# Decoder kernel on one core: the key splits get their own signal, and seven moves in the queues of four engines around attention

## The reference

```
layer 0: causal attention, 16 heads of 128, biases   -> adjacency from ctx (top-k, sigmoid) -> ternary experts, top-1 of 32
layer 1: causal attention, 16 heads of 128, 4 key/value heads, rotary, head_scale -> cross attention with ctx -> 16 experts, top-4, and a shared one

q = rotary(x @ Wq); k = rotary(x @ Wk); v = x @ Wv           # layer 1
attn = softmax(causal(q k^T / sqrt(128))); out = (attn @ v * head_scale) @ Wo
```

## Time and profile before

| | before |
|---|---|
| median of 3 runs | 883.27 us (881.48 to 884.78) |
| the profiled execution: its own time | 881.88 us |
| its span | 880.1 us |
| TensorE busy | 795.0 us (90%), 4727 matmuls |
| VectorE, ScalarE, GpSimd busy | 578.0, 421.4, 500.4 us |
| mean granted TensorE clock | 0.965 |

### The profile page before, as it was taken

How to read it: one execution, slowest core, us unless ns; L and a number is a source line. 1 busy time by engine, 2 the same in 40 slices (tenths; PEclk the granted TensorE clock), 3 DMA queues, 4 the chain that set the end, 5 groups by cost and what they waited for, 6 DMA issues and landing times. The chain is left out here.

```text
span 880.1 us, 14575 instructions
## 1 busy us (share of the span) xinstructions
PE 795.0 (90%) x4727; PEld 681.2 (77%) x4733; DVE 578.0 (66%) x1659; ACT 421.4 (48%) x1193; POOL 500.4 (57%) x409
## 2 busy tenths in 40 slices
PE   7899999999999977594899999999987699999995
PEld 5678888888988866293678788888876488888884
DVE  4796967868668476333688788776726655554555
ACT  5164636546356546061376665765753633223232
POOL 4857287575768441603484566457512376777764
PEclk9999999999999998797999999999999799999998
DMA  6220702204225310564120111010001011111111
GB/s 205 73 96 1 239 20 78 96 1 144 72 73 168 96 54 20 168 157 103 61 74 5 54 54 55 1 55 25 25 1 38 13 38 51 52 38 54 38 40 48
DMA packets 58332, 59.09 MB, mean 67 GB/s; under 512 B 5393, under 2 KB 49313, under 8 KB 58273
## 3 DMA queue, kind: packets, MB, share of 16 engines
q1 hardware_dynamic: 57504, 56.24, 20.5%
q0 software_dynamic: 768, 2.10, 0.7%
HBM read 50.00 MB, written 8.32 MB: 66 GB/s over the span
## 5 line engine op out<-in xcount | busy, mean ns | idle before, releaser
L976 ACT ACTIVATE a_probs<-bank,a_neg_peak 128x128 f32<-128x128 f32 (+1 forms) x256 | 103.2, 429 | 100.5 <-DVE a_neg_peak L1094 100.5
L1004 ACT ACTIVATE a_probs<-a_probs,a_row_inv 128x128 f32<-128x128 f32 (+1 forms) x256 | 92.1, 454 | 6.2 <-DVE a_row_inv L1102 6.2
L1094 DVE CUSTOM_DVE_ANT_0 bank<-bank,causal 128x128 f32<-128x128 f32 (+1 forms) x256 | 82.5, 395 | 15.3 <-PE bank L837 15.3
L982 ACT ACTIVATE a_probs_t<-bank 128x512 f32<-128x512 f32 x96 | 54.1, 602 | 78.8 <-PE bank L857 78.8
L126 PE MATMUL bank<-a_wo_hi,a_ot_hi 128*128 128x256 f32 x256 | 74.6, 291 | 7.9 <-DVE a_ot_lo L1114 7.5
L876 PE MATMUL bank<-a_probs_t,a_vals 128*128 128x256 f32 x256 | 76.6, 381 | 2.7 <-DVE a_ot_lo L1114 2.0
L1814 POOL TENSOR_TENSOR d_h_lo<-d_h,d_h_hi 128x512 fp32r<-128x512 f32 x40 | 51.7, 1294 | 45.6 <-ACT d_h_hi L1934 32.0
L689 POOL TENSOR_TENSOR a_queries<-sim 128x512 f32<-128x512 f32 x32 | 41.5, 1298 | 60.1 <-DVE sim L1069 60.1
L2020 DVE TENSOR_TENSOR d_h<-d_silu,bank 128x512 f32<-128x512 f32 x40 | 27.5, 688 | 71.8 <-PE bank L128 70.5
L127 PE MATMUL bank<-a_wo_lo,a_ot_hi 128*128 128x256 f32 x256 | 73.0, 285 | 0.0
L128 PE MATMUL bank<-a_wo_hi,a_ot_lo 128*128 128x256 f32 x256 | 73.0, 285 | 0.0
(11 more groups left out here) (328 smaller groups left out, 2425.1 us busy)
## 6 DMA issues: line engine op xcount, KB each, us to landing
d_raw<-in_L_ffn_we_dram SPq DMA_DIRECT2D x48, 128.0 KB, 2.2
raw_k<-in_L_attn_w_k_dram SPq DMA_DIRECT2D x8, 512.0 KB, 6.4
raw_q<-in_L_attn_w_q_dram SPq DMA_DIRECT2D x8, 512.0 KB, 5.6
raw_v<-in_L_attn_w_v_dram SPq DMA_DIRECT2D x8, 512.0 KB, 7.2
raw_o<-in_L_attn_w_o_dram SPq DMA_DIRECT2D x8, 512.0 KB, 3.5
kv<-_L_ffn_expert_masks_dram SPq DMA_DIRECT2D x16, 256.0 KB, 3.1
kvt<-_L_ffn_expert_masks_dram SPq DMA_DIRECT2D x16, 256.0 KB, 3.1
raw_o<-in_L_attn_Wo_dram SPq DMA_DIRECT2D x8, 512.0 KB, 3.6
```

Source lines behind the costliest of these rows:

```text
L976: nc.scalar.activation(probs[s % 2][:, i, at:at + width], c.banks[i][:, at:at + width], ACT.Exp, bias=neg_peak[:, n:n + 1], scale=-1.0, ac ...
L982: nc.scalar.activation(probs_t[:, i * BANK:(i + 1) * BANK], c.banks[3 + (3 * s + i) % 2][:], ACT.Copy).then_inc(s_pt_free, 1)
L1004: last = nc.scalar.activation(part, part, ACT.Copy, scale=row_inv[:, s % 2, n + r:n + r + 1])
L1094: last = nc.vector.tensor_tensor_reduce(part, part, mask, -1.0, 3e38, ALU.add, ALU.min, neg_peak[:, n + r:n + r + 1])
```

## The change

1. Layer 1: the key part of a group is split first and alone, with a semaphore of its own, `s_split_k`; the key projection waits only for that.
2. Layer 1: the fourth value tile is projected before `scores(0)` and not behind `proj(1)`, and ScalarE evicts it before `exps(0)`.
3. Layer 1: in steps that still project, one transposed bankful comes before the next projection and two behind it; before it was two and one.
4. Layer 1, VectorE: the addition of the second output bank (u = 1) goes from the end of an odd step to behind `peaks` of the next (not at `TURN_STEP`).
5. Layer 1, VectorE: `sums` runs as two tiles in step 1 and two in step 3, between the two output banks, and no more behind steps 0 and 2; `norm3.apply` goes from the end of step 4 to step 5, behind `peaks(6)` and ahead of `pv(4)`.
6. Both layers, step 14: ScalarE takes the four q = 0 exponentials of step 15 before `pt(14)` and the other four behind `pv(14)`; VectorE takes `inverses(15)` behind `pv(14)`.
7. Both layers: `last_output` waits for the exponentials of the bank that it writes, not for all.

```diff
+        self.s_split_k = S("split_k") if self.rope else None
...
         for n, heads in (("k", min(self.KH, 2)), ("q", 2)):
+            if parts and self.rope:
+                self.split(pool, parts, self.s_split_k)
+                parts = []
...
-                    pe.wait_ge(s_split_proj, s + 1)
...
                         if rope and what == "k":
-                            pe.wait_ge(s_split_proj, group_of(s, what) * STEPS + 1)
+                            pe.wait_ge(weights.s_split_k, group_of(s, what) + 1)
+                        else:
+                            pe.wait_ge(s_split_proj, s + 1)
...
-                    pe.wait_ge(s_exp, PAIRS_OF_HEADS * NT)
                     pe.wait_ge(s_taken, taken("pv", LAST - 1 + (heads.stop - 1) // 2, (heads.stop - 1) % 2))
                     for u in range(2):
+                        pe.wait_ge(s_exp, LAST * NT + B + 2 * u)
...
-                    first_values(range(0, 3))
+                    first_values(range(0, NT // 2))
                 scores(0)
...
-                    first_values(range(3, 4))
...
-                    transposes(s, range(0, 2))
+                    first = 1 if rope and count else 2
+                    transposes(s, range(0, first))
                     proj(s + 2, range(0, min(count, 1)) if late else range(early, count))
-                    transposes(s, range(2, 3))
+                    transposes(s, range(first, 3))
...
-                early = 3 if rope else 0
+                early = NT // 2 if rope else 0
...
+                    if s == LAST - 1:
+                        exps(s + 1, range(0, 1))
                     pt(s)
-                    if s == LAST - 1:
-                        exps(s + 1)
...
-                    if s < LAST - 1 and late:
-                        exps(s + 1)
+                    if s < LAST and late:
+                        exps(s + 1, range(1 if s == LAST - 1 else 0, 2))
...
                     if s < LAST:
                         peaks(s + 1)
+                    if rope and s % STEPS == 0 and s not in (0, TURN_STEP + 1):
+                        output(s // STEPS - 1, 1, ring_bank("o", s // STEPS - 1, 1))
+                    if rope and s == NORM_STEP + 1:
+                        weights.norm3.apply(dve, 1, weights.s_norm3)
...
-                        if s < LAST and not (rope and count):
+                        if s < LAST - 1 and not (rope and count):
                             inverses(s + 1)
                     if not defers(s):
                         pv(s)
...
-                        if s < LAST and count < 3:
-                            inverses(s + 1)
+                    if s == LAST - 1 or s < LAST and late and count < 3:
+                        inverses(s + 1)
...
-                        for u in range(2):
+                        for u in range(1 if rope and s != TURN_STEP else 2):
                             output(s // STEPS, u, ring_bank("o", s // STEPS, u))
-                    if rope and s < NT // 2:
-                        weights.sums(dve, range(NT // 2 + s, NT // 2 + s + 1))
-                    if rope and s == NORM_STEP:
-                        weights.norm3.apply(dve, 1, weights.s_norm3)
+                    if rope and s % STEPS and s < NORM_STEP:
+                        weights.sums(dve, range(NT // 2 + s - 1, NT // 2 + s + 1))
```

More of the change, by code:

```diff
@@ L968, in _, with exps @@
             def _(act):
-                def exps(s):
-                    for q in range(2):
+                def exps(s, halves=range(2)):
+                    for q in halves:
                         for b in range(B):
```

## The result

The changed kernel takes **877.59 us** (median of 6 runs, 875.22 to 879.55); the kernel before, beside it, took 883.87 us (6 runs). The ratio is 0.9927, 95% interval 0.9905 to 0.9950: 6.3 us faster, between 4.4 and 8.4. The forecast was 879.9 us in a range of 876.5 to 883.2. The profiled execution has a span of 875.5 us and a time of its own of 877.31; before it was 880.1 and 881.88.

The account below looks back on a forecast made before the run. TensorE, busy for 90% of the span, was taken as the bound, with gains only where it stands still or runs at half clock. Terms summed to 3.35 us, giving 878.5, plus 1.39 to the median: 879.9 us, range 876.5 to 883.2.

Parts of the forecast that it names:

- The end of layer 1: Step 14, before last_output: wait falls from 3.42 to 1.7 us, clock kept; gain 2.85 us, 1.35 if the clock falls.
- The end of layer 0: End of layer 0's attention: GpSimd finishes last, so the next block begins 0.5 us earlier, bounds 0 and 0.7.
- Key first: Layer 1, steps 1, 3, 9, 11: waits for the query-weight split vanish; 1.7 us in the first two, 1.3 in the others.
- The start: Layer 1, before scores(1): the value tile only moves, wait grows from 1.50 to 3.0 us; gain 0, bounds -0.3 and 0.3.
- a rival with 0.7: Layer 1's start: the 3.0 us wait drops the clock too, costing about 0.7; counted inside the forecast's chance of 0.55.
- Steps 1 to 5: Layer 1: scores(6) comes 1.5 us earlier, step 5 gives it back; gain of all steps up to there 0.2 us.
- -1.5 for the clock: Step 5, behind pv(5): the wait grows from 2.00 to some 3.4 us; half clock costs 1.5, bounds 0 and 1.7.
- The 0.6 charged for the rotation of the keys: Layer 1's moved sums: the first tile runs into the key rotation, VectorE held until GpSimd's instruction ends; 0.6 us charged.
- The reading that VectorE is held by GpSimd's splits: Step 5: norm3.apply's four instructions each wait for one of GpSimd's splits; they took 5.76 us before the change.
- The other rivals of step 5: VectorE not held: 7.3 us gain, 876.0, chance 0.10; held for all of GpSimd's run: slower, 884.5, chance 0.07.
- The clock's rule: TensorE's waits in layer 1: one of 2.00 us left the clock alone, one of 3.42 us did not.
- The sum: Whole kernel: 2.85 + 0.5 + 1.3 + 0 + 0.2 - 1.5 = 3.35 us gained.

Follow-up runs that it names:

- the key's kernel: The kernel before with only the key split first and signalled by itself (item 1); ratio to the kernel before 0.9930.
- the half `keep`: The changed kernel with the first half of layer 0's keep moved ahead, into VectorE's idle time behind peaks(15); ratio to the kernel before 0.9918.
- the four with one part each: The kernel before with one part alone: items 6 and 7, ratio 0.9952; item 1, 0.9930; items 4 and 5, 1.0011; item 2, 1.0011.

## Why the prediction was right, point by point

**The end of layer 1** (2.85 forecast): the wait was to be 1.7 and is 1.61, the clock to be kept and is kept. `transposes(15)` win 2.97 us counted from scores(15), the block 3.22. Right. The runs show what the clock has in it: with the wait of 3.41 and no fall, in the key's kernel, the same stretch takes 23.08 us, so 1.4 of the 3.2 are the wait and 1.85 the clock.

**The end of layer 0** (0.5): 0.63, with GpSimd last, as the steps said. Right, and the half `keep` shows that it was GpSimd: it moves the block by 1.9 us more. The clock fell behind the block's wait, which the forecast didn't name, at no cost.

**Key first** (1.3 in steps 9 and 11): 1.89. The mechanism was right, and the term was sized by the waits alone. In steps 9 and 11 the waits were 1.3 us, and in each of the four steps the gain was about 0.28 more than the wait (1.11 in step 1, where the wait was 0.83). The rows show part of it: in an unbroken run a matmul starts 0.16 us before the record of the one ahead ends (in the key's kernel the key's first starts at 460.83, the query's last ends at 460.99), and behind a wait it doesn't.

**The start** (0, bounds -0.3 and 0.3): this step failed. The wait grew to 2.90 as forecast (3.0), but the clock fell behind it, and scores(1) to (2) lost 1.45 us. It was written down as a rival with 0.7, and a chance of its own inside the forecast; the price was twice that, since no slack of VectorE's chain took anything off. By the runs it happens 4 times in 6.

**Steps 1 to 5** (+0.2, and -1.5 for the clock): from scores(2) to scores(6) 1.92 us were won where 1.5 were forecast. They are the key's alone: the kernel with items 1, 6 and 7 wins 2.20 over the same stretch (54.67 us against 56.87), so the moved sums and additions, to which the forecast gave a part of the 1.5, cost 0.28 here. Counted from scores(2), `peaks(3)` comes 1.11 us earlier with the key and 1.44 with all items, and the addition moved behind it takes 0.68. The 0.6 charged for the rotation of the keys was right in size: L416 took 1.02 us beside it (465.08 to 466.10), where 0.42 is its time, and L418, the one the forecast had in mind, 0.48.

In step 5 `scores(6)` to `pv(5)` took 8.86 us (505.04 to 513.90), where 8.85 were worked out (506.15 to 515.0); L1313 took 4.39 us behind `peaks(6)`, within the "4 to 5 us". Net: 2.93 lost in step 5, 1.0 in all five steps, against 1.3 forecast. The reading that VectorE is held by GpSimd's splits was only argued; the kernel with `norm3.apply` out of their way shows it: 1.38 us for the same four. Read singly in the trace of the changed kernel, they end at 509.34, 511.77, 512.39 and 513.19, each 0.15 us behind the end of one of GpSimd's splits (509.19, 511.62, 512.24, 513.04). The Trainium skill ("SBUF — State Buffer", Who interferes with whom) says that the two engines lock a shared pair of ports against each other for whole instructions; the runs agree: one of the four takes 345 ns without the splits and 1098 beside them, as a quarter of the span of all.

**The other rivals of step 5** fell: VectorE was held, but not for all of GpSimd's run, which goes on to 515.44 in the changed kernel, 2.25 us after L1313's end at 513.19; and the moved additions made no new wait in steps 8, 10 and 12, whose stages are equal.

**The clock's rule was wrong, and its sum came out right.** "A wait of 2.00 us left the clock alone, one of 3.42 did not" took two waits of one execution for a threshold. The table shows none among the waits from 1.97 to 3.50 us: 2.00 us lost the clock in 2 of 5 profiles, and 3.27, 2.90 and 3.41 kept it in some. What the length changes is how often. The Trainium skill ("TensorE: Matmul & The Clock Gate", HAM oscillation) warns of long stretches without matmuls; the trace agrees that the longer ones are the worse ones, but falls behind 2.00 us are more than its warning covers.

**The sum.** 3.35 was forecast and the stages of the two profiles hold 3.38: 0.6 too little for the key, 0.4 for the end of layer 1, 0.4 for other stages, and 1.35 too little loss at the start. That they cancel is chance. The measured gain is 6.3 us, and 6.5 when repeated. Of the 3 us between, 1.7 is that the profiled execution of before was a quick one, and 1.2 lies at other places of the two profiles. Whether the average execution owes these to the change stays open. If the falls are counted by the table and not as they fell in this pair, the stages give about 4.4 us (0.7 more for `pv(5)` before the change, 0.5 less for its end of layer 1, 0.6 and 0.3 more for the two waits of the changed kernel), which leaves 2. One candidate was seen: at the start of layer 0 the kernel before and the four with one part each wait 1.97 to 2.20 us for the keys, all others 1.43 to 1.47, which with its falls would be 1.2 to 1.3 us. It seems to go back to a transfer, behind which GpSimd's run comes 0.5 us later, and a copy of VectorE beside it ends 0.5 us later (L1138, 4.26 us, where the changed kernel's takes 3.62). In all five profiles with the long wait this split waits for the transfer of `raw_k`, in none of the nine others; the row is that of the split in the kernel before:

```profile
28.71 1.04 POOL L449 TENSOR_TENSOR a_wk_hi<-raw_k,one 128x512 fp32r<-128x512 f32 x1 [2.21 <-DMA raw_k<-in_L_attn_w_k_dram]
```

In the changed kernel this split starts at 28.18 and waits for nothing but TensorE. The four ran on one chip and the others elsewhere, so kernel and chip aren't told apart here, and it doesn't fit the key's kernel, which has the long wait and the large gain.

## What to carry to other kernels

A part's gain is best read as the time between two marks of the trace and not as the length of a wait; and a change of seven parts can win in sum while several of them lose: here the key and the ends were worth 10 us and items 2 to 5 cost 2 to 3. Before an instruction of VectorE is moved, look at what GpSimd does at the new place: the same four instructions took 1.38 us at one and 4.39 at another. A granted clock seen once behind a wait is one draw: count it over several profiles before a threshold goes into a sum.

## What was not expected of the hardware

The clock's fall at the same wait in the same kind of kernel isn't fixed: about 2 us of standing still lost it in 4 of 10 cases, 2.90 in 4 of 6, 3.4 in 6 of 8, and 1.29 to 1.64 in none of 42. One fall costs 1.4 to 1.7 us (in step 5 21.35 to 21.63 against 19.97, at the start 11.79 against 10.11), 2.9 where it lasted longer (12.97 at the start), and nothing in the block behind layer 0's attention; so a few of them move a single profile by as much as this whole change. Nor had it been expected that a transfer landing at 28.7 us goes with a longer wait of TensorE ten us later.
